# The order of two loads on the SP queue in a fused attention and FFN layer: zs ahead of x

## What is computed

```python
x = x + _layernorm(attn(_layernorm(x), W_Q, W_K, W_V, W_O, b_Q, b_K, b_V, b_O))
x = x + _layernorm(ffn(_layernorm(x), weight, bias))
# attn: q, k, v per head; causal softmax(q k^T / sqrt(128)) v; out = einsum('bqhe,hed->bqd', z, W_O) + b_O
# ffn:  bw = where(w >= 0, 1, -1) * mean(|w|, per row); einsum('bsi,oi->bso', x, bw) + bias
```

## Time and profile before

| what | value |
|---|---|
| time, two runs | 2770.62 and 2932.45 us, median 2851.53 us |
| the profiled execution, its time | 2774.93 us |
| its span, slowest core (core 7) | 2773.4 us |
| spans of all cores | 2761.8 to 2773.4 us |
| TensorE busy | 1913.8 us, 69% |
| DVE, ACT, POOL busy | 36%, 20%, 9% |

### The profile page before, as it was taken

How to read it: one execution, slowest core, us unless ns; L and a number is a source line. 1 busy time by engine, 2 the same in 40 slices (tenths; PEclk the granted TensorE clock), 3 DMA queues, 4 the chain that set the end, 5 groups by cost and what they waited for, 6 DMA issues and landing times.

```text
span 2773.4 us, 27245 instructions; the slowest of 8 cores (2761.8 to 2773.4 us)
## 1 busy us (share of the span) xinstructions
PE 1913.8 (69%) x8336; PEld 814.5 (29%) x8336; DVE 988.8 (36%) x1760; ACT 554.4 (20%) x737; POOL 239.3 (9%) x558
## 2 busy tenths in 40 slices
PE   2568788778778878878877877436456654665465
PEld 1323233233333323323323323223222222222222
DVE  3533333333333333333333333666322332233323
ACT  1222312321321330331231132100000110011001
POOL 1001111110110111111111111000000000000000
PEclk9679889989989999989989989756778877888778
DMA  6412112112212212212223330530121112111210
GB/s 146 129 18 29 14 20 29 14 22 27 23 12 27 24 14 26 23 17 24 29 45 50 43 53 6 156 106 31 47 68 38 38 38 76 38 39 38 72 43 31
DMA packets 178475, 119.34 MB, mean 43 GB/s; under 512 B 168100, under 2 KB 168100, under 8 KB 170148
## 3 DMA queue, kind: packets, MB, share of 16 engines
q0 software_dynamic: 107200, 75.51, 16.2%
q1 hardware_dynamic: 71140, 42.07, 6.0%
HBM read 125.97 MB, written 25.17 MB: 54 GB/s over the span
## 4 chain that ended last, share of the span: by engine, by line
PE 58%; DVE 11%; ACT 9%; issue 8%; DMA 7%; POOL 3%; DVEq 3%; ACTq 0%; SPq 0%; POOLq 0%
PE psA L362 8%; PE psB L362 8%; PE psE L659 6%; ACT ptil L586 5%; PE psA L747 5%; PE psB L747 5%; PE psC L362 4%; PE psC L856 4%; DVEq L58 3%; PE psC L622 3%; DMA kt<-zs 3%; DMA qt<-zs 3%; POOL ptil L612 2%; PE psE L856 2%; PE psD L856 2%
## 5 line engine op out<-in xcount | busy, mean ns | idle before, releaser
L641 DVE TENSOR_TENSOR ptil<-ptil,c 128x512 bf16<-128x512 bf16 x640 | 220.2, 417 | 480.0 <-ACT c L631 461.6
L362 PE MATMUL psA<-arena_a,wbuf 128*128 128x512 bf16 x1024 | 305.6, 385 | 5.0 <-ACT arena_a L276 3.1
L362 PE MATMUL psB<-arena_a,wbuf 128*128 128x512 bf16 x1024 | 304.0, 384 | 2.8 <-ACT arena_a L276 2.8
L659 PE MATMUL psE<-ptil,v 128*128 128x512 bf16 x640 | 187.6, 389 | 52.4 <-DVE ptil L641 52.4
L622 PE MATMUL psC<-ptil,onem_sb 128*128 128x512 bf16 x640 | 182.6, 399 | 52.1 <-POOL ptil L609 25.2
L586 ACT ACTIVATE ptil<-psA,mbias 128x1024 bf16<-128x1024 f32 x160 | 178.3, 1114 | 183.0 <-PE psE L659 78.0
L747 PE MATMUL psA<-arena_b,qt 128*128 128x512 bf16 x256 | 87.2, 426 | 159.3 <-DMA qt<-zs 159.3
L747 PE MATMUL psA<-arena_b,kt 128*128 128x512 bf16 x256 | 86.2, 422 | 160.5 <-DMA kt<-zs 160.5
L612 POOL TENSOR_TENSOR ptil<-ptil,tri_sb 128x128 bf16<-128x128 bf16 x256 | 108.7, 425 | 890.1 <-ACT ptil L586 890.0
L586 ACT ACTIVATE ptil<-psB,mbias 128x1024 bf16<-128x1024 f32 x160 | 177.2, 1107 | 0.0
L490 ACT ACTIVATE srow<-srow 1x1 f32<-1x1 f32 x32 | 6.5, 202 | 819.8 <-DVE srow L485 819.8
(11 more groups left out here) (125 smaller groups left out, 2270.8 us busy)
## 6 DMA issues: line engine op xcount, KB each, us to landing
c<-fw POOLq DMA_DIRECT2D x16, 1024.0 KB, 6.1
ptil<-x SPq DMA_DIRECT2D x16, 1024.0 KB, 7.0
out<-wbuf POOLq DMA_DIRECT2D x16, 1024.0 KB, 9.4
wbuf<-wq POOLq DMA_DIRECT2D x16, 512.0 KB, 8.4
wbuf<-wk POOLq DMA_DIRECT2D x16, 512.0 KB, 8.4
c<-x SPq DMA_DIRECT2D x8, 1024.0 KB, 5.0
wbuf<-wv POOLq DMA_DIRECT2D x16, 512.0 KB, 8.6
zs<-c SPq DMA_DIRECT2D x64, 128.0 KB, 2.0
```

The lines of the kernel that those rows point to most:

```text
L362: e.matmul(banks[bidx], wslot[sl][:, c * 128:(c + 1) * 128], ln1t3[:, c, s * SLW:(s + 1) * SLW], start=(c == 0), stop=(c == NCH - 1)),
L641: dv_norm[j] = p.op("vector", lambda e, j=j, g=g: e.tensor_tensor(pslot[j], pslot[j], rbc[g % 2], ALU.mult), wait=wait, inc="DV")
L659: pe_av = p.op("tensor", lambda e, j=j, chunks=chunks: e.matmul(psE[:, 0:GQ], v_sb[:, j * 128:(j + 1) * 128], pslot[j], start=(j == 0), st ...
```

## The change

In `emit_front_pe` the two loads change places: the statement that issues zs(i) now stands ahead of the one that issues x(i). Their waits, sizes, buffers and semaphores are the same.

```diff
--- before.py
+++ after.py
@@ -721,12 +721,6 @@
     def emit_front_pe(i):
         nonlocal sc_r2_prev
         par = i % 2
-        wait = [("DV", gp_x3[i - 2])] if i - 2 in gp_x3 else \
-            [("PE", B0_PE), ("DV", B0_DV), ("SC", B0_SC), ("GP", B0_GP),
-             (XAs[3], xa_tot[3])]
-        xc_t[i] = p.op("sync", lambda e, i=i, par=par: e.dma_start(
-            xin[par], x_h.ap()[i * 128:(i + 1) * 128, :]),
-            wait=wait, inc=XCs[par], incn=16)
         wait = [("PE", pe_proj[i - 2])] if i - 2 in pe_proj else \
             [("PE", B0_PE), ("DV", B0_DV)]
         if i < 2:
@@ -735,6 +729,12 @@
         zr_t = p.op("sync", lambda e, i=i, d=zrd: e.dma_start(
             d[:, 0:H * 128].rearrange("p (h q) -> p h q", q=128),
             zs_h.ap()[i].transpose([1, 0, 2])), wait=wait, inc=ZRs[par], incn=16)
+        wait = [("DV", gp_x3[i - 2])] if i - 2 in gp_x3 else \
+            [("PE", B0_PE), ("DV", B0_DV), ("SC", B0_SC), ("GP", B0_GP),
+             (XAs[3], xa_tot[3])]
+        xc_t[i] = p.op("sync", lambda e, i=i, par=par: e.dma_start(
+            xin[par], x_h.ap()[i * 128:(i + 1) * 128, :]),
+            wait=wait, inc=XCs[par], incn=16)
         for hh in range(H):
             for s in range(NPS):
                 wait = []
```

## The result

| | before | changed |
|---|---|---|
| all runs, median | 2772.88 us (10 runs) | 2445.44 us (11 runs) |
| lowest | 2767.65 us | 2421.60 us |
| profiled execution, time | 2774.93 us | 2425.44 us |
| its span | 2773.4 us | 2423.9 us |

The changed kernel takes 0.878 times as long, 95% interval 0.874 to 0.881: 12% faster. The forecast was 2427 us, with a range of 2412 to 2528.

A forecast was written before the change was run, and what follows sets the result against it. TensorE waits for the zs load behind x's wait on SP, a closed loop of 56.45 us a tile. 1936.2 + 13 x 31.4 + 77.9 = 2422.3 us span, plus 1.5 and 3 for edges, gives 2427 us, range 2412 to 2528.

The forecast's parts named there:

- The wait and its cause: Projection's first matmul L747 waits 319.8 us for zs loads, which stand on SP behind x loads waiting for L906.
- TensorE's tile when fed: Projection/FFN loop: projection 14.9 us plus transposes, copy, FFN and bias 16.5, together 31.4 us a tile.
- The edge from FFN to projection: Last L861 to next L747: 0 to 0.44 us a tile extra, 3 us taken for 14 tiles.
- The start: Nothing moves up to the end of FFN 0; projection 2 starts at 1936.2 us instead of 1959.65.
- The end: Start of projection 15 to the end of the span: 80.7 us less 2.8 is 77.9.
- zs in time: zs(i+1), issued after L906 of tile i-2, lands in 10.8 us at the median, 7 to 9 us to spare.
- x: x(i), issued after L906, lands in 7.0 us, 13.8 at most; median 2.9 us before L804 wants it; cost 0.
- the loop through L906: x issue, landing, L804 to L815, copies, L210 to L906: 16.9 us plus landing; passes 31.4 if landing exceeds 14.5.
- rival two: x load becomes the bound in the loop: at 18 us landing, 34.9 us a tile, 2476 us; chance 0.07.
- The clock: TensorE's granted clock in the gapless projection/FFN loop: forecast 1.00, with fed TensorE at that clock given chance 0.54.
- The rival at 0.35: Lowered clock holds through the projection/FFN stage: 37.8 us a tile, 2516 to 2519 us; chance 0.35.
- No change, slower: zs not getting ahead on SP, 2775 us, chance 0.02; x taking 45 us, 2852 us, chance 0.02.

The follow-up runs named there:

- the held-back zs: Changed kernel, but zs(i) also waits for L906 of tile i-2, as x(i) does; 2679.43 and 2695.28 us, ratio to before 0.969.

## Why the prediction was right

*The wait and its cause.* Right. The waits of L747 have gone, and two different ways of sparing zs(i) the wait of x(i) give the same time.

*TensorE's tile when fed, 31.4 us.* Measured 31.43. It was the sum of two stretches that the old trace had at full clock, and it holds with DMA running over it.

*The edge from FFN to projection, 0 to 0.44 us.* Measured 0.31 from start to start, which was in the 31.4 already: the extra is 0, and the 3 us that I carried for it were not there.

*The start.* Projection 2 at 1936.47, worked out 1936.2, and here the agreement is luck. I worked it out on core 7, where tile 0 ran at the lowered clock, and the new profile shows core 3. Tile 0's transposes start 3.6 us later there (1919.82 against 1916.26), and from them to projection 2 it takes 16.65 us at a full clock in place of the 19.9 I had; the two cancel. Core 7 itself, now at a full clock, starts projection 2 at 1927.36.

*The end.* From projection 15 to the end of the span 78.8 us (2345.07 to 2423.9), worked out 77.9. The last FFN still waits 8.01 us for its copy and starts slowly after it (1.01 us for its first pair of matmuls, against 0.59 in a fed tile).

*The sum.* Span 2423.9 measured, 2422.3 worked out: 0.3 from the start, 0.4 from 13 steps, 0.9 from the end. My 2427 stands 3 above the sum for the edges, and the profiled execution took 2425.44. That the loop came out is no luck, 31.43 against 31.4 thirteen times; that the whole is within 2 us is in part that of the start.

*zs in time.* Right: 10.6 and 10.7 us from issue to landing at the median in the loop, as before, with 9 us to spare.

*x.* The experiments gave the slack three pieces, 2.9 + 5.7 + 4.9 = 13.5 us, and their sum is right in size: at a delay of 20.5 us TensorE idles 6.8 more, and 20.5 - 13.5 is 7.0. The pieces one by one are not shown. At 4 us more of delay L804 waits and TensorE does not; at 12.5 the time rises by some 3 us; at 20.5 it is L840, and not L804, that passes the lateness on to TensorE. The other half of that step, that x's landing may take 14.5 us every time before the loop through L906 closes, no run tests: in these three the release was late and not the landing, and it did not hang on L906. The landing of 13.8 us that I took as the longest of x, and as what spoke for rival two, was that of x(1), issued at 1758.88 before the loop; in the loop of before no x took over 9.0 us, and none near 14.5.

*The clock.* The forecast had it at 1.00 and the profiled execution had that on all eight cores. The rival at 0.35 was no phantom: in three of the eight runs that the ratio compares one pair of cores had a mean of 0.89 and the time was 24 to 28 us above the lowest (below). A forecast of 2427 fits the runs without it, and that the profiled one was such a run was not known beforehand.

*No change, slower.* Neither. The wait ahead of zs on SP is met one tile earlier, as the pairs x(2), zs(3) show.

What I had not split was the share of place and of release. Alone, the place ahead of x gives 6.5 of the 25.0 us a tile, since the old loop's 10.8 us of landing hid a queue of its own. In the changed kernel the place is not what counts: zs(i+1) goes out behind x(i) and again lands in 10.6 to 10.7 us, and the tile in advance hides that.

## What to carry to other kernels

SP issued its loads in the order of the code, so a load whose own condition had long been met waited for the condition of the load ahead of it, at 25.0 us a tile. Sort the loads by when they can go, not by when the code thinks of them. Find the closed loop (here: FFN, tail, load, projection, FFN), count how many tiles it spans, and compare its length per tile with the busiest engine's own time: that engine's time is what is left. And ask what a late transfer really delays: x could be issued 12.5 us later for some 3 us in all, because its reader's engine was idle later.

## What the runs showed of the hardware

Two transfers issued some 0.45 us apart share the way: at the median 512 KB of zs took 10.8 us behind 1 MB of x (the kernel before) and 4.3 to 5.7 us ahead of it (the held-back zs), and x 7.0 us ahead of zs and 10.0 behind it. In both kernels a store of 1 MB goes out beside them.

After 7.40 us without a matmul the granted clock was 0.50 for 5 us; that is 1.2 of the 2.4 GHz.

The clock of a gapless stage is not the same in all runs. In the run of 2445.44 us cores 6 and 7 took 2443.7 and 2443.9 us at a mean clock of 0.892, the other six 2415.9 to 2419.3 us at 0.901 to 0.903; in that of 2449.94 us it was cores 2 and 3, with 2448.3 and 2448.4 us. At 6.4 us more for a tile at the lowered clock (37.8 less 31.4, from the trace of before), 27 us are about four tiles; this is an estimate, since these runs have no trace. In the trace of before core 7 had a mean of 0.80 in its first two tiles where core 4 of the same die had 0.93. In smaller windows of that trace cores 6 and 7 read 0.81 from 1905 to 1930 us, and the other six 1.00 from 1910 to 1920; the rest of core 4's 0.93 is its slow start. The Trainium skill ("TensorE: Matmul & The Clock Gate", Part 1, the warning on the peak-current limiter) lets the whole die go down once three of its cores run dense matmuls, and stay down. These readings do not agree with that: two cores of a die went down while its other two ran the same two tiles at 1.00, and in the profiled execution of the changed kernel all eight cores ran the gapless loop for 414 us at 1.00. What decides when it comes was not tried.
